# A fused attention and mixture-of-experts layer on one core: the attention's 32 token blocks split 17 and 15 around the experts instead of 16 and 16

## The chip, the cores and the metric

The kernel runs on one core of a Trainium2 chip, in one launch. The metric is the device time of that execution in microseconds. All data is fp32 but for a few 0/1 tables.

The core's engines run side by side, each through its own instruction list, and wait for each other on semaphores: TensorE (PE in the profile, with PEld for its weight loads), VectorE (DVE), ScalarE (ACT), GpSimd (POOL), and SyncE (SP), which only issues transfers here. ACT and POOL issue transfers too.

## The reference, cut to what matters

```python
x = L0_attn_x                       # 4 x 1024 tokens x 256
xn = _layernorm(x)
x = x + attn(xn) + moe(xn)
...
# attn: 16 heads of 16; each token sees itself and the 127 tokens before it (local),
#       and the means of earlier 16-token chunks (latent, 4 heads of 16)
mixed = gate * local + (1.0 - gate) * remote_h
return mixed @ out_w + out_b
...
# moe: 64 experts, 8 chosen per token, plus one shared expert
hmid = jax.nn.silu(x @ wg) * (x @ wu)
acc + cw[:, None] * (hmid @ wdn)     # for each expert; cw is 0 where it isn't chosen
```

## The kernel before

The 4096 tokens are 32 blocks of 128. Eight blocks make one batch row of 1024 tokens. The program has five parts, and every engine runs through them in the same order.

1. **Opening** (to about 106 us). Layer norm, routing scores, the choice of 8 experts for each token, and for each of the 32,768 (token, place) pairs the slot of a table `slot_rows` in DRAM, where rows lie sorted by expert.
2. **Attention, first part.** `attention(0)`: blocks 0 to 15. Meanwhile GpSimd copies normalised tokens into their slots: `scatter`, 8 indirect transfers for each of the 32 token blocks, 256 in all (line 636). They have a pace of their own (`pace`): before some of them GpSimd waits until the attention has come to a certain head pair, 15 pairs for each 4 token blocks, so 120 pairs in all. An attention block has 8 head pairs.
3. **Experts.** `experts()`: 160 rounds of two 128-row tiles. ScalarE loads the tiles from `slot_rows` (`load_pair`, line 1232) and copies gate and up weights into `wt` (`keep_weights`, line 1228); TensorE transposes the tiles (line 935), multiplies with gate and up (line 951) and with down (line 960); VectorE forms the products; GpSimd sends results to `home_rows` in DRAM, in token order (`send_home`, line 663). The first tile load needs every scatter to have landed, because any tile can hold rows of any token:

```python
for j in range(2):
    act.wait_ge(scattered[j], 16 * K * (NB // 2))
experts()
```

Before the experts VectorE also builds a table of expert numbers (`pair_row`, line 1661) and raises `words_ready`; TensorE and ScalarE wait for it, ScalarE after its first four tile loads and ahead of its first `keep_weights`.

4. **Attention, second part.** `attention(HALF)`: blocks 16 to 31. SyncE first waits for the last `send_home`, then loads 4 token blocks' rows of `home_rows` at a time, 1 MB (8 rows a token) for each token block, into a ring of four places `rows_in` in `shared_mem` (line 472), and announces each on `rows_landed`. VectorE adds them, weighted, to `x_all`: `combine` (line 1598), one instruction for each of a token's 8 rows over 128 tokens, which waits for the one before it of the same token block. 256 such instructions add everything. `add_row` places 16 of them (two token blocks) in each attention block from 17 to 31, two in each of the 8 steps; the closing call adds the last two token blocks. Block 16 adds none.
5. **End.** SyncE stores each token block once its rows and its attention result are added.

One attention block is a `body(i, ...)` on each engine, of 8 steps `s`, one for each pair of heads: TensorE `scores` (line 824, into one of two banks `psS`), VectorE `mask_pair` (lines 1542 and 1544), ScalarE `exps` (line 1116), TensorE `turn_probs` and `values` two and three steps later. Other work hangs on single steps: `project_qk(i + 1)` at 5, `latent_max` at 5 and `latent_out` at 7 on VectorE, `keep_q(i + 1, 0)` at 6. The last pieces of block i run in the first steps of block i + 1: `latent_out_turn(i)` on TensorE (line 876) at step 0, which waits for VectorE's `latent_out(i)` (line 1522), then the gate mix and the output projection. The first block of an attention part has no such tail (`tail=False`), and the call after its last block has nothing else (`live=False`). VectorE starts each block with a copy of the mask (line 1456), which marks its beginning in the trace.

Keys and values of the block before stay in SBUF (`kT`, `va`), and are moved down at each block (`shift_k`, `shift_v`), also over the experts.

## Time and profile before

| | us |
|---|---|
| median of 3 runs (lowest to highest) | 1343.48 (1343.24 to 1344.09) |
| the profiled execution's own time | 1347.35 |
| its span, first to last instruction | 1345.6 |
| TensorE busy | 1241.4 |
| VectorE busy | 958.0 |
| ScalarE busy | 862.1 |
| GpSimd busy | 641.8 |

Durations below are of the one profiled execution, whose own time is 3.87 us above the median of the runs. A start time counts from the first instruction. Where a row of the timeline has a bracket, the engine was idle for so long before it, and the name behind the arrow is what ended that; "issue" means that it waited for nothing that the profile shows. Starts of one instruction can lie a little ahead of the end printed for the one before it on the same engine, since they are pipelined.

### The profile page before, as it was taken

Reading aid. Unit: us, or ns where it says so; the run is one execution under the profiler, and the core shown is the slowest. Engines: PE = TensorE matmul, PEld = TensorE weight load, DVE = VectorE, ACT = ScalarE, POOL = GpSimd, SP = SyncE. Lnnn points to the kernel's source line nnn. Section 1 sums busy time; section 2 is a strip of 40 time slices with the busy share of each in tenths; the row PEclk is TensorE's granted clock in tenths of the full one; section 3 lists DMA queues with packets and bytes.
Section 4 is the critical chain, followed back from the end, with each engine's and each line's share of the span. In section 5 each row is a group of like instructions: output and inputs, shape, how many; then the busy total and the mean of one; then the engine's idle time right before and its main releaser. Section 6 shows DMA issues by size and latency. Waiting matters only on the chain.

```text
span 1345.6 us, 38714 instructions
## 1 busy us (share of the span) xinstructions
PE 1241.4 (92%) x9265; PEld 1169.6 (87%) x9267; DVE 958.0 (71%) x4532; ACT 862.1 (64%) x2383; POOL 641.8 (48%) x747
## 2 busy tenths in 40 slices
PE   3948999999999299999999999999999999999996
PEld 3837999999999199999999999999989898999985
DVE  6986666666666157666767676665568898989897
ACT  2416877777778165656556565666667777777774
POOL 7914777777777646656566565665620000000000
PEclk9978999999999699999999999999999999999998
DMA  8106465553333357777777777765543333323330
GB/s 252 64 34 268 165 213 182 188 184 133 120 120 109 128 168 222 227 223 228 217 235 218 216 218 229 228 197 173 169 165 106 106 105 105 105 105 107 109 119 33
DMA packets 152813, 218.40 MB, mean 162 GB/s; under 512 B 24769, under 2 KB 124866, under 8 KB 147650
## 3 DMA queue, kind: packets, MB, share of 16 engines
q1 hardware_dynamic: 80450, 86.77, 20.2%
q0 software_dynamic: 28800, 86.54, 16.8%
q10 hardware_dynamic: 43520, 44.57, 13.1%
q8 instruction: 19, 0.31, 0.1%
q14 instruction: 24, 0.20, 0.0%
HBM read 113.86 MB, written 103.81 MB: 162 GB/s over the span
## 4 chain that ended last, share of the span: by engine, by line
PE 69%; DVE 15%; issue 6%; DMA 4%; ACTq 2%; DVEq 1%; POOL 1%; ACT 1%; SPq 1%; POOLq 0%
PE psS L951 19%; PE psS L824 10%; PE psT L935 5%; PE psO L960 5%; PE psM L960 4%; PE psT L838 4%; DVE x_all L1598 4%; DMA pr<-slot_rows 3%; PE psQ L771 2%; PE psV L782 2%; PE psQ L792 2%; PE psV L811 2%; PE psT L852 2%; PE psT L851 2%; PE psT L850 1%
## 5 line engine op out<-in xcount | busy, mean ns | idle before, releaser
L951 PEld LDWEIGHTS psS<-sm,wt 128*128 128x128 f32 x2560 | 309.9, 193 | 18.6 <-issue 7.5
L951 PE MATMUL psS<-sm,wt 128*128 128x128 f32 x2560 | 315.8, 277 | 1.0 <-issue 0.2
L636 POOL DMA_INDIRECT slot_rows<-x_out_st,idx_st x256 | 256.1, 1000 | 78.6 <-issue 66.3
L1116 ACT ACTIVATE pr<-sm,nmax 128x192 f32<-128x192 f32 x512 | 205.1, 449 | 53.9 <-DVE nmax L1544 52.3
L824 PE MATMUL psS<-kT,qz 128*128 128x192 f32 x1024 | 226.3, 345 | 10.8 <-DVE qz L1487 8.4
L663 POOL DMA_INDIRECT home_rows<-qz,row_idx x160 | 154.7, 967 | 130.2 <-DVE qz L1631 101.4
L1228 ACT COPY wt<-shared_mem 128x512 f32 x320 | 183.3, 626 | 24.6 <-issue 24.6
L663 POOL DMA_INDIRECT home_rows<-sm,row_idx x160 | 155.2, 970 | 82.5 <-issue 44.4
L824 PEld LDWEIGHTS psS<-kT,qz 128*128 128x128 f32 x1024 | 165.3, 193 | 18.3 <-issue 10.7
L1216 ACT ACTIVATE prT<-psS 128x256 f32<-128x256 f32 x160 | 61.6, 385 | 185.5 <-issue 98.0
L1544 DVE CUSTOM_DVE_ANT_0 sm<-psS,pr 128x192 f32<-128x192 f32 x512 | 162.0, 354 | 23.5 <-issue 19.6
L1124 ACT COPY prT<-psT 128x384 f32<-128x384 f32 x256 | 121.9, 476 | 77.7 <-PE psT L838 74.6
L1624 DVE TENSOR_TENSOR prT<-psS,prT 128x256 f32<-128x256 f32 x160 | 67.7, 423 | 105.0 <-ACT prT L1216 104.1
L838 PE MATMUL psT<-ident,pr 128*128 128x128 f32 x768 | 125.9, 273 | 1.2 <-ACT prT L1124 1.2
L1598 DVE SCALAR_TENSOR_TENSOR x_all<-shared_mem,w,x_all (+1 forms) x256 | 123.0, 480 | 0.8
L838 PEld LDWEIGHTS psT<-ident,pr 128*128 128x128 f32 x768 | 99.9, 141 | 7.4 <-issue 2.0
L1210 ACT COPY sm<-psT 128x512 f32<-128x512 f32 x160 | 93.6, 585 | 10.5 <-PE psT L935 5.6
L935 PE MATMUL psT<-ident,pr 128*128 128x128 f32 x480 | 74.2, 278 | 24.9 <-DMA pr<-slot_rows 24.5
L1542 DVE MEMSET met<- 1x1 f32 x256 | 15.1, 59 | 100.7 <-PE psS L824 90.0
L1487 DVE TENSOR_TENSOR qz<-qT,own_head 128x1024 f32<-128x1024 f32 x64 | 78.2, 1221 | 7.3 <-ACT qT L1050 7.3
L960 PE MATMUL psO<-shared_mem,prT 128*128 x320 | 82.5, 381 | 0.2 <-DVE prT L1624 0.2
L960 PE MATMUL psM<-shared_mem,prT 128*128 x320 | 82.4, 380 | 0.0
(283 smaller groups left out, 2472.8 us busy)
## 6 DMA issues: line engine op xcount, KB each, us to landing
shared_mem<-home_rows SPq DMA_DIRECT2D x32, 1024.0 KB, 5.1
pr<-slot_rows ACTq DMA_DIRECT2D x120, 272.0 KB
qz<-slot_rows ACTq DMA_DIRECT2D x40, 272.0 KB
slot_rows<-wt SPq DMA_DIRECT2D x32, 272.0 KB
shared_mem<-in_L_ffn_We_gate SPq DMA_DIRECT2D x64, 128.0 KB
shared_mem<-in_L_ffn_We_up SPq DMA_DIRECT2D x64, 128.0 KB
shared_mem<-in_L_ffn_We_down SPq DMA_DIRECT2D x64, 128.0 KB
x_all<-in_L_attn_x SPq DMA_DIRECT2D x4, 1024.0 KB, 9.7
```

What stands on the lines that cost most here:

```text
L636: pool.indirect_dma_start(slot_rows, bass.IndirectOffsetOnAxis(ap=idx_st[:, j, k:k + 1], axis=0), x_out_st[:, j % 2, :], None).then_inc(sc ...
L663: pool.indirect_dma_start(home_rows, bass.IndirectOffsetOnAxis(ap=row_idx[:, j, a:a + 1], axis=0), ys[j][:, a, :], None).then_inc(y_out[j] ...
L824: last = mm(psS[:, p % 2, u * WIN:(u + 1) * WIN], qz[:, c, u, heads, :].rearrange("p h t -> p (h t)"), kT[:, c, u * UQ:u * UQ + WIN], star ...
L838: last = nc.tensor.transpose(psT[:, 0, a * P:(a + 1) * P], flat[:, a * P:(a + 1) * P], ident[:])
L935: last = nc.tensor.transpose(psT[:, j % 2, (a * DC + c) * P:(a * DC + c + 1) * P], xs[j][:, a, c * P:(c + 1) * P], ident[:])
L951: last = mm(psS[:, j % 2, (2 * a + n) * P:(2 * a + n + 1) * P], wt[j % 2][:, a, c, n * F:(n + 1) * F], xsT[:, j % 2, a, c, :], start=(c == ...
L960: last = mm((psM, psO)[j % 2][:, a * D:(a + 1) * D], hT[:, j % 2, a, :], ring_d[:, e % RING, :], start=True, stop=True)
L1116: nc.scalar.activation(pr[:, p % 4, par, :], sm[:, p % 4, par, :], ACT.Exp, bias=nmax[:, p % 4, par:par + 1], scale=-1.0).then_inc(probs, 1)
L1124: nc.scalar.copy(prT[:, p % 2].rearrange("p a t -> p (a t)"), psT[:, 0, 0:3 * P]).then_inc(prT_ready, 1)
L1228: last = nc.scalar.copy(wt[j % 2][:, a, :, :], ring_gu[:, e % RING, :, :])
L1544: v.tensor_tensor_reduce(sm[:, p % 4, u, :], psS[:, p % 2, u * WIN:(u + 1) * WIN], mask[:, u * WIN:(u + 1) * WIN], -1.0, -FLOOR, ALU.add, ...
L1598: ins = v.scalar_tensor_tensor(x_all[:, t, :], row, w8[:, t, k:k + 1], x_all[:, t, :], ALU.mult, ALU.add)
```

## The change

The constant HALF = 16 becomes FIRST = 17, and `attention` on TensorE, ScalarE and VectorE is given its first and last block: 0 to 16 in front of the experts, 17 to 31 behind them. The waits at the end of the first part count 17 blocks' pairs. SyncE's and GpSimd's programs are the same as before.

Blocks 18 to 31 and the closing call now have room for 30 of the 32 token blocks' rows. So block 17, the first behind the experts, adds the rows of two token blocks (0 and 1) in its last four steps: 16 instructions, four in each step, where block 16 added none. (Token block t's rows are added in the same attention block as before for every t.)

```diff
-HALF = NB // 2
+FIRST = NB // 2 + 1
...
-            def attention(start):
+            def attention(start, end):
...
-                with pe.Fori(start + 2, start + HALF - 1) as i:
+                with pe.Fori(start + 2, end - 1) as i:
                     body(i, 2)
-                body(start + HALF - 1, 2, ahead=False)
-                body(start + HALF, 2, live=False)
-                out_project(start + HALF - 1)
+                body(end - 1, 2, ahead=False)
+                body(end, 2, live=False)
+                out_project(end - 1)
...
-            attention(0)
+            attention(0, FIRST)
             pe.wait_ge(words_ready, 1)
             pe.sem_inc(pairs_done, 1)
             experts()
-            attention(HALF)
+            attention(FIRST, NB)
...
-            act.wait_ge(masked, 2 * HALF * NPAIR)
-            act.wait_ge(pv_pair, HALF * NPAIR)
+            act.wait_ge(masked, 2 * FIRST * NPAIR)
+            act.wait_ge(pv_pair, FIRST * NPAIR)
...
+                    if resuming and s >= NPAIR // 2:
+                        for n in range(2):
+                            add_row(i, 4 * s - 2 * NPAIR + n)
                     if combining:
                         add_row(i, 2 * s)
...
+                    if resuming and s >= NPAIR // 2:
+                        for n in range(2, 4):
+                            add_row(i, 4 * s - 2 * NPAIR + n)
                     if combining:
                         add_row(i, 2 * s + 1)
...
             def add_row(i, n):
-                combine(2 * (i - HALF - 1) + n // K, 2 * ((i + 1) % 2) + n // K, (n % K,))
+                combine(2 * (i - FIRST) + n // K, 2 * ((i + 1) % 2) + n // K, (n % K,))
...
-                body(start, 0, nth, tail=False, resuming=combining)
-                body(start + 1, 1, max(nth, 1), last_tail=False, combining=combining)
-                with dve.Fori(start + 2, start + HALF - 1) as i:
+                body(start, start % BPS, nth, tail=False, resuming=combining)
+                body(start + 1, start % BPS + 1, max(nth, 1), last_tail=False, combining=combining)
+                with dve.Fori(start + 2, end - 1) as i:
```

In the instruction lists TensorE, ScalarE, GpSimd and SyncE have the same rows as before; only loop bounds and awaited counts differ. VectorE's list differs in the first attention block behind the experts. There, step 5 stood so before (line 1542 and the four rows behind it are `mask_pair`, `small` and `lmax` are `latent_max`):

```order
L1542 MEMSET met 1x1
L1544 ISA sm,nmax<-psS,pr 128x192
L1544 ISA nmax 128x1
L1544 ISA sm,nmax<-psS,pr 128x192
L1544 ISA nmax 128x1
L1508 TENSOR_TENSOR small<-psM,lat_wide 128x256
L1511 TENSOR_REDUCE lmax<-small 128x4
L1513 SCALAR_TENSOR_TENSOR small<-lmax,small 128x256
```
And in the kernel after the change, with the four rows that end step 4 ahead of it:

```order
L1604 SCALAR_TENSOR_TENSOR x_all<-shared_mem,w,x_all 128x256 x4
L1542 MEMSET met 1x1
L1544 ISA sm,nmax<-psS,pr 128x192
L1544 ISA nmax 128x1
L1544 ISA sm,nmax<-psS,pr 128x192
L1544 ISA nmax 128x1
L1604 SCALAR_TENSOR_TENSOR x_all<-shared_mem,w,x_all 128x256 x2
L1508 TENSOR_TENSOR small<-psM,lat_wide 128x256
L1511 TENSOR_REDUCE lmax<-small 128x4
L1513 SCALAR_TENSOR_TENSOR small<-lmax,small 128x256
L1604 SCALAR_TENSOR_TENSOR x_all<-shared_mem,w,x_all 128x256 x2
```
The added rows (line 1604 is what was line 1598) stand ahead of `latent_max` and behind it. Step 7 of the same block, up to the mask copy that opens the next block, stood so before:

```order
L1542 MEMSET met 1x1
L1544 ISA sm,nmax<-psS,pr 128x192
L1544 ISA nmax 128x1
L1544 ISA sm,nmax<-psS,pr 128x192
L1544 ISA nmax 128x1
L1518 TENSOR_SCALAR lden<-psM 128x4
L1520 RECIPROCAL lrec<-lden 128x4
L1522 TENSOR_TENSOR lat<-psM,lrec 128x64
L1456 COPY pr<-masks 128x384
```
And after the change:

```order
L1542 MEMSET met 1x1
L1544 ISA sm,nmax<-psS,pr 128x192
L1544 ISA nmax 128x1
L1544 ISA sm,nmax<-psS,pr 128x192
L1544 ISA nmax 128x1
L1604 SCALAR_TENSOR_TENSOR x_all<-shared_mem,w,x_all 128x256 x2
L1518 TENSOR_SCALAR lden<-psM 128x4
L1520 RECIPROCAL lrec<-lden 128x4
L1522 TENSOR_TENSOR lat<-psM,lrec 128x64
L1604 SCALAR_TENSOR_TENSOR x_all<-shared_mem,w,x_all 128x256 x2
L1456 COPY pr<-masks 128x384
```
Two added rows stand ahead of `latent_out` (`lden`, `lrec`, `lat`), and two behind it.

## Rows read from the trace of the kernel before

**Rows 1.** Page, part 1: busy time, share of the span and instructions of each engine.
```profile
...
PE 1241.4 (92%) x9265; PEld 1169.6 (87%) x9267; DVE 958.0 (71%) x4532; ACT 862.1 (64%) x2383; POOL 641.8 (48%) x747
...
```

**Rows 2.** Windows: length, each engine's busy us (instructions), granted clock, DMA share, GB/s.
```profile
...
376.24:397.28 21.04, 20.84 (x157) 19.89 (x156) 13.76 (x63) 16.35 (x54) 16.43 (x19) 1.00 0.34 119
449.10:470.10 21.00, 0.00 (x0) 0.00 (x0) 0.24 (x1) 0.00 (x0) 12.47 (x13) 0.56 0.34 118
470.10:475.60 5.50, 5.50 (x25) 5.25 (x26) 0.74 (x7) 4.44 (x7) 0.00 (x0) 0.50 0.31 105
1157.02:1178.68 21.66, 21.04 (x157) 19.86 (x156) 19.41 (x79) 16.20 (x54) 0.00 (x0) 1.00 0.33 109
...
```

**Rows 3.** Timeline, VectorE (start, length, instruction, idle before): mask copies, two blocks in front.
```profile
...
376.24 0.60 DVE L1456 COPY pr<-masks 128x384 f32 x1 [0.50 <-issue]
...
397.28 0.60 DVE L1456 COPY pr<-masks 128x384 f32 x1 [0.50 <-issue]
```

**Rows 4.** Timeline, VectorE: mask copies of two blocks behind the experts.
```profile
...
1157.02 0.36 DVE L1456 COPY pr<-masks 128x384 f32 x1 [0.24 <-issue]
...
1178.68 0.36 DVE L1456 COPY pr<-masks 128x384 f32 x1 [0.24 <-issue]
```

**Rows 5.** Timeline, all engines: from the front attention's end to the experts' start.
```profile
...
445.35 0.37 ACT L1101 COPY mixedT<-psV 128x256 f32<-128x256 f32 x1 [1.70 <-PE psV L803]
...
448.66 0.42 DVE L1535 TENSOR_TENSOR x_all<-psV,x_all 128x256 f32<-128x256 f32 x1 [3.93 <-PE psV L812]
449.00 0.34 DVE L1661 SCALAR_TENSOR_TENSOR pair_row<-expert_row 1x192 int32<-1x192 int32 x1
...
464.46 0.96 POOL L636 DMA_INDIRECT slot_rows<-x_out_st,idx_st  x1 [0.30 <-issue]
467.06 1.49 ACTq L1232 DMA_DIRECT2D pr<-slot_rows  x3
468.58 0.49 ACTq L1232 DMA_DIRECT2D qz<-slot_rows  x1
...
470.10 1.97 PE L935 MATMUL psT<-ident,pr 128*128 128x128 f32 x8 [21.48 <-DMA pr<-slot_rows]
470.14 1.14 ACT L1228 COPY wt<-shared_mem 128x512 f32 x2 [24.42 <-issue]
...
```

**Rows 6.** Timeline, TensorE: the experts' first 16 gate and up matmuls.
```profile
...
471.90 3.78 PE L951 MATMUL psS<-sm,wt 128*128 128x128 f32 x16
...
```

**Rows 7.** Line 636, GpSimd's scatters, from 140 to 448 us.
```profile
...
L636 POOL DMA_INDIRECT slot_rows<-x_out_st,idx_st x231: 956/960/2002, 139.3 to 446.8; - x116
...
```

**Rows 8.** The same line from 449 to 467 us.
```profile
...
L636 POOL DMA_INDIRECT slot_rows<-x_out_st,idx_st x13: 956/960/961, 449.3 to 464.5; - x13
...
```

**Rows 9.** Timeline, VectorE: second half of block 16, then block 17's mask copy.
```profile
...
998.28 0.35 DVE L1544 CUSTOM_DVE_ANT_0 sm<-psS,pr 128x192 f32<-128x192 f32 x1 [1.44 <-issue]
...
1001.71 0.35 DVE L1544 CUSTOM_DVE_ANT_0 sm<-psS,pr 128x192 f32<-128x192 f32 x1 [1.55 <-issue]
...
1003.50 1.23 DVE L1487 TENSOR_TENSOR qz<-qT,own_head 128x1024 f32<-128x1024 f32 x1 [1.14 <-ACT qT L1050]
...
1005.61 0.23 DVE L1522 TENSOR_TENSOR lat<-psM,lrec 128x64 f32<-128x64 f32 x1
1005.75 0.35 DVE L1456 COPY pr<-masks 128x384 f32<-128x384 f32 x1
...
```

**Rows 10.** Timeline, VectorE: block 17's first two added rows, and its third pair.
```profile
...
1006.70 1.00 DVE L1598 SCALAR_TENSOR_TENSOR x_all<-shared_mem,w,x_all 128x256 f32<-128x256 f32 x2
...
1011.37 0.35 DVE L1544 CUSTOM_DVE_ANT_0 sm<-psS,pr 128x192 f32<-128x192 f32 x1 [1.14 <-issue]
...
```

**Rows 11.** Line 472: issue to landing of the load issued at 989.56 us.
```profile
...
DMA to landing us min/median/max: 4.9/4.9/4.9
```

**Rows 12.** The same of the load issued at 989.98 us.
```profile
...
DMA to landing us min/median/max: 7.5/7.5/7.5
```

**Rows 13.** Line 876, TensorE behind the experts: what ended its idle time (us, times).
```profile
...
  DVE lat L1522: 11.9, 30
...
```

More of the change, by code:

```diff
@@ L1190, in body, with attention @@
                         keep_qk(i + 1, 0, 2)
-            def attention(start):
+            def attention(start, end):
                 nth = min(start, 2)
@@ L1199, in attention @@
                 body(start + 1, max(nth, 1))
-                with act.Fori(start + 2, start + HALF - 1) as i:
+                with act.Fori(start + 2, end - 1) as i:
                     body(i, 2)
-                body(start + HALF - 1, 2, ahead=False)
-                body(start + HALF, 2, live=False)
+                body(end - 1, 2, ahead=False)
+                body(end, 2, live=False)
             def keep_tiles(j, u, first):
@@ L1261, in experts @@
                     step(j, PAIRS // XS - 1, MANY, named, final=True)
-            attention(0)
-            act.wait_ge(masked, 2 * HALF * NPAIR)
-            act.wait_ge(pv_pair, HALF * NPAIR)
+            attention(0, FIRST)
+            act.wait_ge(masked, 2 * FIRST * NPAIR)
+            act.wait_ge(pv_pair, FIRST * NPAIR)
             act.wait_ge(cleared, 16 * (E // ZROWS))
@@ L1271, in _ @@
             act.wait_ge(pairs_done, PAIRS + 1)
-            attention(HALF)
+            attention(FIRST, NB)
         @block.vector
@@ L1599, in combine, with attention @@
                     ins.then_inc(combine_steps if k < K - 1 else combined, 1)
-            def attention(start, combining):
+            def attention(start, end, combining):
                 nth = min(start, 2)
@@ L1608, in attention @@
                     dve.wait_ge(gu_ready, PAIRS)
-                body(start, 0, nth, tail=False, resuming=combining)
-                body(start + 1, 1, max(nth, 1), last_tail=False, combining=combining)
-                with dve.Fori(start + 2, start + HALF - 1) as i:
+                body(start, start % BPS, nth, tail=False, resuming=combining)
+                body(start + 1, start % BPS + 1, max(nth, 1), last_tail=False, combining=combining)
+                with dve.Fori(start + 2, end - 1) as i:
                     body(i, i % BPS, 2, combining=combining)
-                body(start + HALF - 1, BPS - 1, 2, ahead=False, combining=combining)
-                body(start + HALF, None, 2, live=False, closing=combining)
+                body(end - 1, (end - 1) % BPS, 2, ahead=False, combining=combining)
+                body(end, None, 2, live=False, closing=combining)
                 if combining:
                     dve.wait_ge(combined, NB)
-                accumulate(start + HALF - 1)
+                accumulate(end - 1)
             def make_h(j, u, first):
@@ L1676, in _ @@
             dve.wait_ge(x_biased, NB)
-            attention(0, False)
-            dve.wait_ge(probs, 2 * HALF * NPAIR)
-            dve.wait_ge(pv_pair, HALF * NPAIR)
+            attention(0, FIRST, False)
+            dve.wait_ge(probs, 2 * FIRST * NPAIR)
+            dve.wait_ge(pv_pair, FIRST * NPAIR)
             experts()
@@ L1687, in _ @@
             dve.wait_ge(weights_kept, 1)
-            attention(HALF, True)
+            attention(FIRST, NB, True)
 _INS = ['L0_attn_x', 'L0_attn_qkv_w', 'L0_attn_qkv_b', 'L0_attn_rq_w', 'L0_attn_rq_b', 'L0_attn_rkv_w', 'L0_attn_rkv_b',
```

## The prediction

> **What bounds the kernel now.** I read the page's busy times first. TensorE is busy 1241.4 us of the 1345.6 [rows 1], so about 104 us of its time are idle, and the question is which of it lies where the change acts. Then I took windows of one block in front, one behind, and of the stretch between the first attention part and the experts [rows 2]. In front TensorE is busy 20.84 of 21.04 us and VectorE 13.76: the block is TensorE's, and VectorE has some 7 us to spare. Behind, TensorE shows 21.04 and VectorE 19.41 of 21.66. From 449.1 to 470.1 TensorE and ScalarE do nothing, VectorE 0.24 us, and only GpSimd works.
>
> The mask copies give the length of a block exactly: 397.28 - 376.24 = 21.04 us in front [rows 3] and 1178.68 - 1157.02 = 21.66 us behind [rows 4].
>
> The timeline of the gap [rows 5] says what it waits for. VectorE adds block 15's result at 448.66. GpSimd's scatters go on until 464.46 + 0.96 = 465.42. At 467.06 ScalarE issues the experts' first tile loads, and the tile is there at 470.10, where TensorE ends an idle time of 21.48 us. So the gap isn't attention and isn't experts: it is the end of GpSimd's own queue. From 449 to 467 us there are 13 scatters with 960 ns each as median [rows 8].
>
> **Part 1: one more block in front.** It costs 21.04 us [rows 3] on all three engines, and it is put into a gap of 21.48 us [rows 5]. GpSimd's list is not changed, and its pacing asks for 120 head pairs, which the first 15 blocks deliver, so block 16 never holds it. What matters is which of the events that start the experts comes last now.
>
> - ScalarE's last attention copy ends at 445.35 + 0.37 = 445.72; plus 21.04 that is 466.76, before the 467.06 at which it issued tile loads.
> - The scatters now run beside a working attention to their end. There the median is 960 ns as well [rows 7], but with longer spells between: 231 starts from 139.3 to 446.8 us are 1.34 us apart, 13 starts from 449.3 to 464.5 us are 1.27 apart [rows 7, 8]. For 13 scatters that is 0.9 us: last scatter over at 466.3, tile loads from 468.0, all four issued (they took until 468.58 + 0.49 = 469.07 before [rows 5]) at 470.0, tile there at 471.0.
> - VectorE's last addition starts at 448.66 + 21.04 = 469.70, and `pair_row` [rows 5], right behind it, ends at 449.00 + 0.34 + 21.04 = 470.38. ScalarE waits for that word now, which before had been there for 20 us. It then needs what it needed before between its last load and its first weight copy, 470.14 - 469.07 = 1.07 us: 471.45 instead of 470.14, 1.31 late.
>
> So the word, not the scatters, comes last, and the first gate and up matmuls move from 471.90 [rows 6] to 473.2. Against it stands TensorE's clock. After the long pause those 16 matmuls took 3.78 us [rows 6], in a stretch with a granted clock of 0.50, which is 1.2 GHz [rows 2]. In the changed kernel TensorE comes from the attention's end with a pause of 1 to 2 us. At 2.4 GHz the set takes half, 1.9 us less, which is more than the 1.3 lost; but ScalarE's own start is 1.3 late too, so not more than that can be won back. Both ends: 0 and +1.3. I take +0.8, a little nearer to the loss, since the attention's drain has waits of its own and may leave the clock low.
>
> **Part 2: one block less behind.** That removes a steady block, 21.66 us [rows 4], since the fill, the first blocks and the closing call stay as they are. The load of rows, the additions per token block and the stores are the same work.
>
> **Part 3: 16 additions in the first block behind.** Two in a row took 1.00 us [rows 10], so 16 are 8.0 us of VectorE. In block 16, whose place block 17 takes, VectorE idled before the pair of step 5 for 1.44 us, before that of step 6 for 1.55, and before `keep_q` for 1.14 [rows 9]. Followed through: four additions in step 4 take 2.0, less 1.44: 0.56 late. Four in step 5: 0.56 + 2.0 - 1.55 = 1.01 late. In step 6 the first two lie in the wait before `keep_q`; but that wait is for ScalarE, which follows the late mask pair, so 1.01 stays; the two behind it make 2.01. In step 7 two stand ahead of `latent_out`, which ends 3.01 late; two more behind it make 4.0 at the next mask copy (at 1005.75 before [rows 9]).
>
> Who waits for VectorE there? TensorE's turn of the latent result (line 876), with the rest of the block's first step queued behind it: behind the experts its idle time was ended by `lat` 30 times, TensorE and weight loads together, 11.9 us in all [rows 13]. This is where each block ties TensorE to VectorE, so TensorE is 3.0 late. The last 1.0 falls into the idle 1.14 before the next block's third pair [rows 10]. I take +3.0. Below stands 0, if TensorE has work ahead of it at each point; above 8.0, if nothing is covered.
>
> The rows must be there in time. The first two loads took 4.9 and 7.5 us [rows 11, 12] from 989.56 and 989.98: landed at 994.5 and 997.5. Token block 0 is wanted at the end of step 4's pair, 998.28 - 1.44 = 996.8 [rows 9], token block 1 in step 6, after 1001.7. No wait.
>
> **Sum.** +0.8 - 21.66 + 3.0 = -17.9 us. Against the span: 1345.6 - 17.9 = 1327.7; the execution's own time goes from 1347.35 to 1329.5. The runs' median was 3.87 below that execution: 1343.48 - 17.9 = 1325.6.
>
> **The rivals.**
> - *The additions are not covered.* The lateness spreads into TensorE and ScalarE, and all 8.0 us count: -21.66 + 8.0 + 0.8 = -12.9, 1330.6 us. For it: the steps tie three engines together in both directions. Against it: the idle times [rows 9]. 12%.
> - *The additions are absorbed.* TensorE turns out to be bound in this block by its own work and 0 to 1 us remains: 1322.6 to 1323.6. For it: TensorE shows 20.84 of 21.04 us busy in a block in front [rows 2]. Against it: the tie at `lat`. 12%.
> - *The scatters grow longer beside a working VectorE.* Their longest in the attention was 2002 ns [rows 7], 1.04 over the median. If each of the 13 took that, the last would end 13.5 us later, and the experts would start 13.5 late: 13.5 - 21.66 + 3.0 = -5.2, 1338.3 us. Against it: the median in the attention equals the one in the gap. 6%.
> - *The other side: the scatters follow the attention.* If the queue's end is tied to the attention's end in a way that the pacing's numbers don't show, the gap stays: +21.04 - 21.66 + 3.0 = +2.4, 1345.9 us, slower than before. It decides from 18.7 us of added delay at the last scatter on. The change would then not do what it does on paper. For it: GpSimd does wait for attention events in places. Against it: 1.27 us from scatter to scatter with nothing else running shows a queue bound by itself. 3%.
> - *A new wait in the experts' first rounds,* some 5 to 8 us, 1331 to 1334: 5%.
>
> The third rival is a rule of the Trainium skill. Its page "SBUF — State Buffer", section "SBUF: two separate sides", says that VectorE and GpSimd share a port pair as an exclusive lock, and that a transfer issued from GpSimd's queue can't get its descriptors written while certain VectorE instructions run; it gives about 620 ns alone and about 3100 ns overlapped. By those figures 13 scatters would be late by some 32 us, an estimate from that page, and the kernel slower. The trace speaks against it here: 960 ns beside VectorE at 13.76 of 21.04 us busy, and 960 ns beside an idle VectorE.
>
> **How the numbers follow.** My forecast gets 62%; its own range is 1323.3 to 1327.6 (0 to 1.3 in part 1, 1.5 to 4.5 in part 3). The rivals on both sides of it reach to 1322.6 and 1330.6; with a little for another execution that makes 1321.0 to 1331.5, which leaves out the last three rivals. A time within 0.2% (2.7 us, about what a measurement of this kernel can tell from no change) needs the fourth rival: 2%. Slower by more needs it with more on top: 2%. Faster: 96%.
>
> **What the changed profile would show.** TensorE's idle time before its first line 935 instruction falls from 21.48 to about 1 us; the last scatter ends at 466 to 467 us, before the attention's last addition near 469.7; the first weight copy starts near 471.4, with `pair_row` just ahead of it; the first 16 line 951 matmuls start near 473.2, and their length says what the clock did. Behind, the first block is about 4 us longer from mask copy to mask copy than block 16 was, TensorE idles at `lat` at its end, and there is one steady block of 21.66 less. I'm wrong if scatters end after 470 us, if VectorE waits for rows in that block, or if the expert rounds are slower than before.

## The result, and the profile after

| | before | after |
|---|---|---|
| median, us (lowest to highest, 7 runs each) | 1344.79 (1343.24 to 1349.17) | 1332.89 (1329.77 to 1338.67) |
| the profiled execution's own time | 1347.35 | 1338.67 |
| its span | 1345.6 | 1336.9 |

The ratio is 0.9918 (0.9899 to 0.9937): 11.9 us faster, where 17.9 were forecast. 1332.89 us lies above the range of 1321.0 to 1331.5. The forecast of 1325.6 started from 1343.48, the median of the first 3 runs of before; over 7 runs it is 1344.79, so 1.3 of the 7.3 us that are missing lie in the starting point and 6.0 in the change.

The boundary looks as forecast in form. Timeline of the changed kernel, all engines, from the front attention's end to the experts' first rounds; it answers to [rows 5, 6]:
```profile
...
470.12 0.96 POOL L636 DMA_INDIRECT slot_rows<-x_out_st,idx_st  x1 [0.30 <-issue]
...
478.18 0.42 DVE L1535 TENSOR_TENSOR x_all<-psV,x_all 128x256 f32<-128x256 f32 x1 [4.17 <-PE psV L812]
478.52 0.34 DVE L1667 SCALAR_TENSOR_TENSOR pair_row<-expert_row 1x192 int32<-1x192 int32 x1
...
479.00 1.94 PE L935 MATMUL psT<-ident,pr 128*128 128x128 f32 x8 [0.86 <-DVE pair_row L1667]
479.93 1.14 ACT L1228 COPY wt<-shared_mem 128x512 f32 x2 [4.77 <-issue]
...
481.61 3.78 PE L951 MATMUL psS<-sm,wt 128*128 128x128 f32 x16 [0.67 <-ACT sm L1210]
...
486.03 2.77 PE L951 MATMUL psS<-sm,wt 128*128 128x128 f32 x16
```
The wait of 21.48 us is gone. The last scatter ends at 471.08, 7.1 us ahead of VectorE's last addition; the word `pair_row` comes last, and the first weight copy starts 1.75 us behind the addition's start. The whole row of events stands some 8 us later than forecast (the addition was expected near 469.7). That began in the opening, whose program the change doesn't touch. Windows of the opening and of the boundary of the changed kernel:
```profile
...
36.00:60.00 24.00, 23.30 (x115) 23.30 (x116) 14.81 (x22) 8.48 (x15) 23.41 (x33) 0.52 0.26 88
...
474.10:480.10 6.00, 4.68 (x14) 3.23 (x15) 0.68 (x2) 0.54 (x2) 0.00 (x0) 0.50 0.60 182
480.10:487.80 7.70, 7.04 (x33) 6.63 (x33) 1.81 (x15) 6.16 (x11) 0.00 (x0) 0.50 0.01 3
...
```
TensorE was granted 0.52 in the first stretch and got through 115 matmuls. The same window of the kernel before and of `e13_after_again`, a second profile of the changed kernel:
```profile
...
36.00:60.00 24.00, 23.25 (x201) 22.45 (x201) 23.62 (x28) 11.04 (x22) 23.55 (x26) 1.00 0.26 88
...
36.00:60.00 24.00, 24.00 (x152) 24.00 (x152) 16.52 (x23) 9.81 (x18) 23.54 (x30) 1.00 0.26 89
...
```
Here the matmuls say more than the granted clock. Eight of line 696 take 1.00 us in the kernel before and 1.81 in the changed one; in `e13_after_again` they take 1.81 as well until 51 us, though the record shows 1.00 throughout. The first mask copy followed at 114.63 us in the changed kernel (115 matmuls in this window), at 110.10 in `e13_after_again` (152) and at 106.41 in the kernel before (201): slow matmuls here go with a late start of the attention. `e1_before_again`, the kernel before itself, got through 131 and had its mask copy at 115.35, so a late start doesn't need the change.

At the boundary the clock is at its lower level, 1.2 GHz, through the first set of gate and up matmuls (3.78 us) and into the second (2.77 us, granted 0.69; a set takes 1.95 at 2.4 GHz).

VectorE behind the experts, answering to [rows 9, 10] (mask copies and `lat`), and TensorE's wait for `lat` [rows 13]:
```profile
...
997.41 0.35 DVE L1456 COPY pr<-masks 128x384 f32<-128x384 f32 x1
...
1017.81 0.22 DVE L1522 TENSOR_TENSOR lat<-psM,lrec 128x64 f32<-128x64 f32 x1
...
1018.87 0.35 DVE L1456 COPY pr<-masks 128x384 f32<-128x384 f32 x1
...
1038.56 0.35 DVE L1456 COPY pr<-masks 128x384 f32 x1
...
```
```profile
...
1018.09 0.33 PE L876 MATMUL psM<-ident,lat 128*128 128x128 f32 x1 [1.62 <-DVE lat L1522]
...
```
The first block behind takes 21.46 us where block 16 took 18.62: 2.84 more (4.0 forecast). VectorE waited for no rows in it, as forecast. The second takes 19.69 where 20.85 stood, so 1.16 comes back. Steady blocks are the same, 21.66 (answering to [rows 4]):
```profile
...
1104.05 0.36 DVE L1456 COPY pr<-masks 128x384 f32 x1 [0.25 <-issue]
1125.71 0.36 DVE L1456 COPY pr<-masks 128x384 f32 x1 [0.24 <-issue]
...
```
From the first mask copy to the end these two executions take 1239.2 and 1222.3 us: 16.9 less, near the forecast of 17.9. So three things are to be explained: the opening, what a typical execution of the kernel before looks like, and the rest.

### The profile page after: what moved, and what is told of

Its sections match the earlier page's. It is cut to its first block, busy times and chain, and to the rows that moved or that the text cites. A ratio compares the mean times of both kernels' runs of the same rounds, so it can differ in the third digit from the quotient of the medians.

```text
span 1336.9 us, 38681 instructions
## 1 busy us (share of the span) xinstructions
PE 1255.4 (94%) x9266; PEld 1182.4 (88%) x9267; DVE 953.3 (71%) x4532; ACT 861.7 (64%) x2383; POOL 638.7 (48%) x747
## 3 DMA queue, kind: packets, MB, share of 16 engines
q0 software_dynamic: 28800, 86.54, 16.9%
q10 hardware_dynamic: 43520, 44.57, 13.1%
## 4 chain that ended last, share of the span: by engine, by line
PE 73%; DVE 12%; issue 6%; DMA 3%; ACTq 2%; ACT 2%; DVEq 1%; SPq 1%
PE psS L951 19%; PE psS L824 10%; PE psT L935 5%; PE psO L960 5%; PE psT L838 4%; PE psM L960 4%; DVE x_all L1604 4%; DMA pr<-slot_rows 2%; PE psQ L771 2%; PE psV L811 2%; PE psV L782 2%; PE psQ L792 2%; PE psT L852 2%; PE psT L851 2%; PE psT L850 1%
## 5 line engine op out<-in xcount | busy, mean ns | idle before, releaser
L1542 DVE MEMSET met<- 1x1 f32 x256 | 15.1, 59 | 104.4 <-PE psS L824 93.8
```

## The experiments

Eight of the runs (e1 to e8) fell in a condition in which even the kernel before takes 1561 to 1581 us; they are compared only with each other. They come last here. The chip of e5 to e8 is also that of e9 to e15, so it isn't one of a certain chip. "This condition" below is the other one, in which the kernel before takes some 1345 us.

### The same kernel again, and the additions alone

`e13_after_again` is the changed kernel as it is. 

> The changed kernel, unchanged, on the same chip as the others of this call. Theory C: in the kernel before the wait ahead of the experts varies from execution to execution (21.5 us in the profiled one, 18.2 in the kernel with only the additions moved), and the moved block costs its 21.04 + 1.75 less that wait; the typical gain is 15 us, ratio 0.988 to 0.990. Theory A alone (only the changed kernel's opening was unlucky): 17 to 18 us, ratio 0.986 to 0.988.

1333.33 us against 1345.65, ratio 0.9908 (0.9878 to 0.9938): the gain repeats, and so does its size. Theory A (17 to 18 us) falls; the 15 us of theory C are more than the 12.3 measured too. What the clock takes, in the experts' first sets and behind the additions, comes out further down. In its profile the first mask copy is at 110.10, and from addition to weight copy pass 1.74 us.

`e9_additions_alone` keeps 16 blocks in front and 16 behind, and lets block 16 add 16 rows (block 17 none):
```diff
+                    if resuming and s >= NPAIR // 2:
+                        for n in range(2):
+                            add_row(i + 1, 4 * s - 2 * NPAIR + n)
...
-                body(start + 1, 1, max(nth, 1), last_tail=False, combining=combining)
+                body(start + 1, 1, max(nth, 1), last_tail=False)
```


> The kernel before (16 and 16 blocks) with block 17's 16 additions moved into the second half of block 16, block 17 adding none: the third part of the change alone. Read from the mask copies that open blocks 16, 17 and 18, 18.6 and 20.85 us apart in the kernel before. Forecast's chain (late by 4.0 at the next mask copy, 3.0 for TensorE): 22.6, then 19.7 less the 1.0 that is absorbed, sum 41.4. What the changed kernel's profile suggests (its blocks 17 and 18 took 21.45 and 19.69, with additions in both): 21.4, then 18.6 to 19.7. If the additions were absorbed: 18.6 to 19.5 for the first. Ratio 1.000 within 0.001 in each case.

Ratio 1.0023 (1.0006 to 1.0039). The two first blocks behind take 21.71 and 20.09 us, 41.80 against 39.47; the forecast's chain gave 22.6 and 18.8, so its sum (41.4) came near and its parts didn't. Part 3 alone costs 2.3 us in the trace, between "absorbed" and the 3.0 taken. A part of that is TensorE's clock. TensorE now waits 1.61 us for block 16's `lat`, where it waited for nothing before, and right behind it, over the first 3 us of block 17, the granted clock is 0.50 (1.00 in the kernel before):
```profile
...
1007.08:1010.08 3.00, 3.00 (x12) 2.79 (x12) 1.95 (x13) 2.14 (x8) 0.00 (x0) 0.50 0.61 112
...
```
Its boundary gave the clue to the failed term:
```profile
...
450.31 0.42 DVE L1535 TENSOR_TENSOR x_all<-psV,x_all 128x256 f32<-128x256 f32 x1 [3.92 <-PE psV L812]
...
468.48 2.02 PE L935 MATMUL psT<-ident,pr 128*128 128x128 f32 x8 [18.21 <-DMA pr<-slot_rows]
468.66 1.14 ACT L1228 COPY wt<-shared_mem 128x512 f32 x2 [21.37 <-issue]
...
```
Nothing was changed ahead of this place, and the wait is 18.2 us, not 21.48; from addition to weight copy 18.35 us. `e11` and `e15` below show 18.35 and 18.36.

`e10_latent_first` moves the two additions of step 7 from ahead of `latent_out` to behind it:
```diff
-                    if resuming and s >= NPAIR // 2:
+                    if resuming and NPAIR // 2 <= s < 7:
...
-                        for n in range(2, 4):
+                        for n in range(0 if s == 7 else 2, 4):
```


> The changed kernel with all four additions of step 7 of block 17 behind latent_out, where two stood ahead of it. Forecast's chain (TensorE waits for lat, so each addition ahead of it costs its full 0.5 us): the two blocks from mask copy to mask copy, 21.45 and 19.69, sum 41.14 in the changed kernel, become about 40.2. Rival (TensorE's own work or the mask pairs bound this place): the sum stays at 41.1. The ratio is that of the changed kernel.

TensorE's wait for `lat` fell from 1.62 us to 0.69:
```profile
...
1008.62 0.33 PE L876 MATMUL psM<-ident,lat 128*128 128x128 f32 x1 [0.69 <-DVE lat L1522]
...
```
The two blocks take 21.57 and 19.70 us, 41.27 against 41.15: no gain. The clock stays at 1.00 in both executions, and there the tie at `lat`, on which the forecast hung its 3.0, isn't what the additions cost. Whether the shorter wait also spares the fall of the clock that most other executions show (further down) can't be told from one profile. The run's 1331.45 (0.9901, 0.9879 to 0.9923) can't be told from the changed kernel.

### What sets the start of the experts in the kernel before

`e15_no_pacing` is the kernel before without the two lines that pace the scatters. 

> The kernel before (16 and 16) without the waits that pace GpSimd's scatters. Their idle time for attention events was 11.1 us from 140 to 448 us. If the pacing is what makes the scatters late, the last scatter ends up to 11 us earlier, the wait ahead of the experts falls from 18 to 21 us to 8 to 12, and the kernel gains 8 to 11 us, ratio 0.992 to 0.994, by which most of the change's gain would be had without moving a block. Rival (GpSimd is bound by its own 1.27 us for each scatter and catches up after each wait): the last scatter ends within 2 us of before, ratio 0.999 to 1.001.

1345.44 against 1345.65 (0.9995, 0.9979 to 1.0011): the rival held. The last scatter ends at 463.90, where `e9_additions_alone`, with the pacing, has 463.94: the scatters are bound by their own queue, not by the pacing. (Most follow each other in 1.27 us, which makes 325 us for 256; the other 15 us or so are some 30 longer steps.) The rows of the last one and of the start (here line 634 is the scatter):
```profile
...
462.94 0.96 POOL L634 DMA_INDIRECT slot_rows<-x_out_st,idx_st  x1 [0.30 <-issue]
...
468.63 1.14 ACT L1226 COPY wt<-shared_mem 128x512 f32 x2 [21.38 <-issue]
...
```
462.94 + 0.96 = 463.90, and 4.73 us later the first weight copy, as in every profile of this condition with 16 blocks in front (4.72 to 4.74). So the wait is the distance between two chains, the scatters' and the attention's, and that is set where they leave the opening. Kernel before, GpSimd's last tail clearing (line 646) and first scatter, and VectorE's first mask copy:
```profile
...
105.46 1.86 POOL L646 DMA_INDIRECT slot_rows<-shared_mem,tail_idx  x1 [0.30 <-DVE slot_idx L1442]
123.05 1.37 POOL L610 COPY idx_st<-slot_idx 128x8 uint32<-128x8 uint32 x2 [15.73 <-issue]
125.11 0.99 POOL L636 DMA_INDIRECT slot_rows<-x_out_st,idx_st  x1 [0.69 <-issue]
...
106.41 0.35 DVE L1456 COPY pr<-masks 128x384 f32<-128x384 f32 x1
...
```
The same of `e15_no_pacing`:
```profile
...
105.55 0.95 POOL L644 DMA_INDIRECT slot_rows<-shared_mem,tail_idx  x1 [0.30 <-issue]
123.09 0.32 POOL L610 COPY idx_st<-slot_idx 128x8 uint32<-128x8 uint32 x2 [16.58 <-DMA slot_rows<-shared_mem,tail_idx]
124.10 0.99 POOL L634 DMA_INDIRECT slot_rows<-x_out_st,idx_st  x1 [0.69 <-issue]
...
108.21 0.35 DVE L1454 COPY pr<-masks 128x384 f32<-128x384 f32 x1
...
```
GpSimd waits some 16 us for the cleared rows to land. In the profile of before the first scatter follows the first mask copy by 18.70 us; here by 15.89, and in no other profile of this condition by less than 15.1 or more than 16.7. Of the 2.8 us between these two executions 1.8 are an earlier attention (106.41 against 108.21) and 1.0 a later scatter (125.11 against 124.10). From first to last start the scatters then take 338 to 340 us, and the 16 blocks 342, so what differs there stays.

`e17_before_late_scatters` and `e18_after_late_scatters` test this in both kernels: GpSimd clears an unread tile 14 times ahead of its last 8 scatters.
```diff
+        unread = sb("unread", [P, 64])
...
+                if last:
+                    for _ in range(14):
+                        after(nc.gpsimd.memset(unread[:], 0.0))
```


> The kernel before, but GpSimd clears an unread 128x64 tile 14 times ahead of the last 8 scatters: some 3.1 us more in its queue (eight clears of 128x32 took 1.64 us in the opening). Nothing else. Theory A (the start of the experts follows the last scatter in the kernel before, and what varies from execution to execution is the distance between this chain and the attention's): first weight copy 4.7 us behind the last scatter, as in every profile of a 16/16 split, and 21.4 us instead of 18.35 behind the attention's last addition; time +3 us, ratio 1.002 to the kernel before. Rival (the start follows from something else, and the scatters end early enough): 18.35 us stays and the distance to the last scatter falls to 1.6 us; ratio 1.000.

> The changed kernel with the same 14 clears ahead of the last 8 scatters. Theory A: the changed kernel's start of the experts follows the word pair_row behind the attention, and its scatters end some 4.1 us earlier than they need (8.8 us ahead of the first weight copy, where 4.7 would do). So 3.1 us more change nothing: first weight copy still 1.75 us behind the attention's last addition, distance to the last scatter 5.7; ratio about 0.991, as without the clears. Rival (the scatters are still part of what the changed kernel waits for): 1.75 grows to up to 4.9, ratio up to 0.9935.

Before with late scatters: 1350.17 against 1345.81, ratio 1.0030 (1.0016 to 1.0044). The clears and the start of the experts:
```profile
...
455.65 2.88 POOL L631 MEMSET unread<- 128x64 f32 x14
459.47 0.96 POOL L640 DMA_INDIRECT slot_rows<-x_out_st,idx_st  x1 [0.94 <-POOL unread L631]
...
468.32 0.96 POOL L640 DMA_INDIRECT slot_rows<-x_out_st,idx_st  x1 [0.30 <-issue]
...
474.01 1.97 PE L939 MATMUL psT<-ident,pr 128*128 128x128 f32 x8 [21.89 <-DMA pr<-slot_rows]
...
```
The next scatter starts 4.77 us behind the one ahead of the clears (454.70) instead of 1.27, 3.5 late, and the wait is 3.5 longer than 18.35: 21.85 from addition to weight copy, which is 4.73 behind the last scatter. The kernel before follows its scatters, one for one.

The changed kernel with the same clears: 1331.62, ratio 0.9892 (0.9875 to 0.9910), no loss. Last scatter, addition, word, first transposes and first weight copy:
```profile
...
467.60 1.16 POOL L640 DMA_INDIRECT slot_rows<-x_out_st,idx_st  x1 [0.30 <-issue]
...
472.10 0.43 DVE L1539 TENSOR_TENSOR x_all<-psV,x_all 128x256 f32<-128x256 f32 x1 [4.17 <-PE psV L816]
472.44 0.34 DVE L1671 SCALAR_TENSOR_TENSOR pair_row<-expert_row 1x192 int32<-1x192 int32 x1
...
473.34 1.97 PE L939 MATMUL psT<-ident,pr 128*128 128x128 f32 x8 [1.28 <-DMA pr<-slot_rows]
473.84 1.14 ACT L1232 COPY wt<-shared_mem 128x512 f32 x2 [4.76 <-issue]
...
```
1.74 us from addition to weight copy, as without the clears. TensorE now waits for the tile again, 1.28 instead of 0.86: from the last scatter's end to the weight copy 5.08 us are left, where 4.73 is the least seen and 8.8 stood without the clears, so the 3.5 us have used up nearly all of the scatters' slack. The rival (the scatters still count) falls for this kernel, and the theory of two chains holds for both.

### The word earlier, and the opening filled

`e14_word_early` is the changed kernel with `pair_row` built ahead of the front attention; it depends on the opening alone.
```diff
             dve.wait_ge(x_biased, NB)
+            dve.wait_ge(experts_known, 16 * QT)
+            by_pair = expert_row[:].rearrange("p (u a) -> p u a", a=2)
+            v.scalar_tensor_tensor(pair_row[:], ...).then_inc(words_ready, 1)
             attention(0, FIRST)
```


> The changed kernel with the experts' number table computed ahead of the first attention part, no filling. The changed kernel starts its weight copies 1.75 us after its last front addition starts, and would start them at 0 without the word. Forecast's theory: 1.3 to 1.9 us less at the first weight copy, up to 4 us less by the third round, since TensorE's clock is better placed (3.9 us in the filled pair); ratio lower than the changed kernel's by 0.001 to 0.003. Rival: the scatters or the tile loads take the place of the word, under 0.5 us.

1330.03, ratio 0.9886 (0.9850 to 0.9923), 3.3 below the changed kernel on the same chip. The two intervals overlap, but its four runs (1328.47 to 1331.94) all lie below the five of `e13_after_again` (1332.16 to 1334.22). Its boundary:
```profile
...
471.18 1.91 PE L935 MATMUL psT<-ident,pr 128*128 128x128 f32 x8
471.33 1.14 ACT L1228 COPY wt<-shared_mem 128x512 f32 x2 [2.93 <-issue]
471.42 0.42 DVE L1535 TENSOR_TENSOR x_all<-psV,x_all 128x256 f32<-128x256 f32 x1 [4.17 <-PE psV L812]
...
473.00 2.33 PE L951 MATMUL psS<-sm,wt 128*128 128x128 f32 x16
...
475.61 1.95 PE L951 MATMUL psS<-sm,wt 128*128 128x128 f32 x16
...
```
The weight copy now starts 0.09 us ahead of the addition: 1.84 won. TensorE's higher clock comes sooner as well: the granted clock is 0.88 over the first set, where the changed kernel has 0.50, and the first two sets take 2.33 and 1.95 us instead of 3.78 and 2.77. The word did come last in the changed kernel.

`e11_before_filled` and `e19_after_filled` fill TensorE's idle time in the opening with transposes that nobody reads, meant to keep its clock up there; `e20_word_early_filled` has both edits.
```diff
+            def fill_time(n):
+                for _ in range(n):
+                    nc.tensor.transpose(psV[:, 384:512], ident[:], ident[:])
...
+            fill_time(12)
...
+                if m in (4, 5, 8):
+                    fill_time({4: 4, 5: 4, 8: 20}[m])
...
+            fill_time(32)
...
+                    fill_time(24)
```


> The kernel before with TensorE's filled opening (as in the second filled run), hoped for on a chip in the condition in which the kernel before takes 1344. Theory C (the experts of the kernel before wait for the scatters, whose chain leaves the opening by another way than the attention): filling helps the attention's start and not the scatters', so the experts start no earlier: from the end of the last front block to the first weight copy 18 to 24 us, ratio 0.998 to 1.001. Theory A alone: ratio 0.995 to 0.998.

> The changed kernel with TensorE's idle stretches of the opening filled with idle transposes into an unread bank, so that its clock doesn't fall there. The same filling did nothing for the 16/16 split (1344.74 against 1345.65). Theory B (the changed kernel's time follows the attention chain out of the opening, whose length hangs on TensorE's clock there, whereas the kernel before follows the scatter chain): the first mask copy at 107.5 to 109 us, the runs narrower than the changed kernel's 1329.8 to 1338.7, median 1329 to 1332, ratio 0.988 to 0.9905. Rival (the opening is not what spreads the changed kernel's times, or the filling costs as much as it gives): median 1333 or more, ratio 0.991 or more, as wide.

> The changed kernel with both: the word pair_row built before the attention and the opening filled. If the two are independent: the 3.3 us that the early word gave in the other kernels (1330.03 against 1333.33) on top of what the filling gives; 1326 to 1330, ratio 0.986 to 0.989. If the filling gives nothing: as the early word alone, 1330, ratio 0.9886.

| | us (lowest to highest) | ratio | first mask copy | first two blocks behind |
|---|---|---|---|---|
| e11_before_filled | 1344.74 (1343.71 to 1345.75) | 0.9988 (0.9968 to 1.0007) | 107.89 | 19.00 + 20.85 |
| e19_after_filled | 1333.39 (1328.85 to 1335.63) | 0.9902 (0.9882 to 0.9921) | 107.51 | 21.85 + 22.89 |
| e20_word_early_filled | 1330.04 (1327.98 to 1332.28) | 0.9882 (0.9865 to 0.9899) | 106.39 | 21.84 + 22.89 |

The filling gives nothing in either kernel, and `e20` comes out as the early word alone: theory C of `e11` held, my expectation for `e19` fell, although the opening was short. The profile shows where a part of it went: the second block behind takes 22.89 us, not 19.69. Windows of its beginning in `e19_after_filled`:
```profile
...
1010.62:1017.00 6.38, 6.38 (x25) 5.67 (x25) 4.45 (x17) 3.52 (x12) 0.00 (x0) 0.53 0.54 185
...
```
And the same place in `e13_after_again`, from the same mask copy:
```profile
...
1013.45:1020.00 6.55, 6.55 (x49) 6.27 (x49) 6.26 (x26) 5.51 (x18) 0.00 (x0) 1.00 0.54 185
...
```
With a granted clock of 0.53 TensorE does 25 matmuls where it does 49 at 1.00. Both executions wait 1.61 us for `lat` just before; in one the clock then falls, in the other it doesn't. Taken over all profiles: where the additions lie in the first block behind and TensorE waits 1.6 us for its `lat`, the clock over the next 3 us is 0.50 to 0.68 in ten of twelve; where it waits 0.69 us (`e10_latent_first`) or not at all (the seven without moved additions), it is 1.00 in all eight. Over the twelve profiles with 17 blocks in front (both conditions) this second block takes 19.7 us three times, 21.3 five times and 22.7 to 22.9 four times. In seven profiles with 16 in front and no moved additions it takes 20.84 to 20.86, every time.

### Where a front block is longer

In e1 to e8 a front block takes 28.3 to 29.0 us in the mean of a profile, and a steady one behind 21.66. Mask copies of `e1_before_again`, the kernel before as it is, in front and behind:
```profile
...
407.31 0.40 DVE L1456 COPY pr<-masks 128x384 f32 x1 [0.50 <-issue]
435.62 0.36 DVE L1456 COPY pr<-masks 128x384 f32 x1 [0.50 <-issue]
...
1392.43 0.36 DVE L1456 COPY pr<-masks 128x384 f32 x1 [0.24 <-issue]
1414.08 0.36 DVE L1456 COPY pr<-masks 128x384 f32 x1 [0.24 <-issue]
...
```
Its list of waits from 250 to 500 us names "remote" as what ended them:
```profile
...
ACT prT L1124 <- remote: 47.0, 16, 5.1
...
DVE met L1542 <- remote: 33.1, 11, 5.6
...
```
The three numbers are us in all, times, and the longest. Over the eight profiles there are 122 to 147 such waits each, the longest 15.2 us, and none at all in the other condition. All of them lie between the first scatter and 3 us behind the last result sent, and none between the last scatter (and 3 us behind it) and the first result: only where GpSimd issues indirect transfers. What holds the engines isn't shown, and I leave it open. With such blocks the attention ends after the scatters already with 16 blocks:
```profile
...
581.72 0.42 DVE L1535 TENSOR_TENSOR x_all<-psV,x_all 128x256 f32<-128x256 f32 x1 [4.17 <-PE psV L812]
...
583.47 1.14 ACT L1228 COPY wt<-shared_mem 128x512 f32 x2 [4.76 <-issue]
...
```
There is no wait to fill: it is 1.75 us already, as in the changed kernel. But the moved block doesn't cost 28 us either. It is the last of the front part, and by then the scatters are over. In `e2_after_again` the last one starts at 555.07; mask copies of blocks 15 and 16:
```profile
...
550.75 0.36 DVE L1456 COPY pr<-masks 128x384 f32 x1 [0.50 <-issue]
...
572.17 0.36 DVE L1456 COPY pr<-masks 128x384 f32<-128x384 f32 x1
...
```
Block 15 takes 21.42 us here (20.5 to 21.8 in the five profiles with 17 in front), and from block 16's mask copy to its addition 30.6 to 30.9 us pass in both conditions. So the moved block costs some 21 us in front and saves 21.66 behind, and what is left is the additions: the first two blocks behind take 43.3 us in the mean of these five against 39.5. (`e3`, `e6` carry the filling, `e4`, `e7` the change and the filling, `e8` the early word on top of these. In `e3` and `e4` the third stretch of the filling has 90 transposes instead of 32.)

> The kernel before, unchanged, as the yardstick for the opening (all up to the first mask copy, 106.4 us in the profiled execution of before, 114.6 in that of the changed kernel). Theory A (the shortfall is chance in the opening: executions of one program are granted TensorE's higher clock for more or less of it): ratio 1.000 within 0.003, runs spread over some 5 us, and the first mask copy may start anywhere from 104 to 115 us. Rival B (the changed program itself starts later): the first mask copy stays at 106 to 107.

> The changed kernel, unchanged. Theory A: the same attention, expert and attention stretches as before (from the first mask copy to the end 1222 us, against 1239), while the first mask copy can stand anywhere from 104 to 115 us; ratio between 0.987 and 0.993 by that chance. Rival B: the first mask copy near 114 again, ratio 0.992.

> The kernel before with TensorE kept busy in the opening by transposes of the identity that nobody reads, put where it waits anyway. Theory A: granted clock 1.0 from about 20 us on, first mask copy at 104 to 107 us, runs within 2 us of each other, ratio 0.996 to 1.000. Rival B: no less spread and the same opening as without.

> The changed kernel with the same filling. Theory A: same opening as the filled kernel of before, so that the two filled kernels differ by the change alone: 17 us (from their profiles 16 to 18), ratio 0.984 to 0.988. Rival B: the changed program still opens some 5 us or more later than the filled kernel of before, and the two differ by 11 to 12 us.

> The changed kernel, unchanged, once more, in the hope of a chip on which the kernel before takes 1344 us (on the chip of the first four runs it took 1577, with front blocks of 28 us in place of 21, so that the gap ahead of the experts was gone). Theory A (gain 17 us behind the opening, opening by chance): from the first mask copy to the end 1222 us; opening anywhere from 104 to 115. Rival B (the changed program opens later): first mask copy near 114.

> The kernel before with the filling, the second stretch of it (which had held TensorE 3 us too long) cut from 90 to 32 transposes. Theory A: first mask copy at 104 to 108 us, ratio 0.996 to 1.000 and less spread from run to run. Rival B: no change in spread.

> The changed kernel with the same filling. Theory A: same first mask copy as the filled kernel of before within 1 us, ratio lower than that one's by 0.0125 (17 us), where front blocks take 21 us. Rival B: first mask copy 5 us or more behind it, ratio lower by only 0.008. If the chip is again one with front blocks of 28 us, both theories say that the moved block costs 28 - 22 = 6 us more in front than behind, and the ratio is higher than the filled kernel of before's by 0.003 to 0.005.

> The filled changed kernel with the experts' number table (the word that ScalarE and TensorE wait for) computed ahead of the first attention part. Forecast's theory (the word is the last event ahead of the experts, 1.3 us behind the old order): TensorE's first tile transposes move up by 0.9 us and ScalarE's first weight copy by 1 to 1.8, the first round's ends by 1 to 1.5; ratio lower by 0.001. Rival (the scatters come last even so): no change.

| | us | ratio to the kernel before |
|---|---|---|
| e1_before_again | 1580.93 | 1.0016 (0.9998 to 1.0034) |
| e2_after_again | 1583.29 | 1.0023 (1.0001 to 1.0045) |
| e3_before_filled | 1579.55 | 1.0017 (0.9995 to 1.0039) |
| e4_after_filled | 1585.05 | 1.0046 (1.0025 to 1.0068) |
| e5_after_again | 1564.88 | 1.0027 (1.0011 to 1.0043) |
| e6_before_filled | 1557.44 | 0.9988 (0.9970 to 1.0006) |
| e7_after_filled | 1564.06 | 1.0014 (0.9993 to 1.0035) |
| e8_word_early | 1561.29 | 1.0002 (0.9983 to 1.0020) |

The change gains nothing there: against the partner with 16 in front its ratio is 0.001 to 0.003 higher. The terms above give -0.6 for the block and +3.9 for the additions, +3.3 us or 0.002, which fits. The 6 us that the expectation of `e7` put on the block were a wrong step, though its sign came out. Whether the kernel loses there isn't settled: the intervals of `e2` and `e5` lie above 1, but `e1`, the kernel before against itself, came out at 1.0016. The gains expected for `e2`, `e4` and `e5` didn't come, nor did the narrower spread expected of the filling (13.0 us from lowest to highest in `e3`, 11.2 in `e6`, 11.4 in `e1`). The early word again moves the weight copy from 1.75 us behind the addition to 0.09 ahead.

## Why the prediction was right or wrong

**The gap was the scatters', and a block fits into it: right.** e17 and e18 show it from both sides.

**Scatters beside a working attention: right.** The last 19 have a mean of 959 ns in the changed kernel, and no scatter of any profile took more than 2.01 us. The rival from the Trainium skill, page "SBUF — State Buffer", section "SBUF: two separate sides" (the port lock, some 3100 ns overlapped), doesn't show in any of these scatters.

**Word last: right.** Forecast 471.45 − 469.70 = 1.75 us from addition to weight copy, measured 1.75.

**+0.8 for the start of the experts: wrong, and this is the step that failed.** It compared the changed kernel with the one profiled execution of before, whose wait of 21.48 us I took as typical and corrected only by "the runs' median was 3.87 below that execution". That offset was not spread evenly. In the profiled execution the attention had left the opening 1.8 us earlier than in `e15` and the scatters 1.0 later, and so the wait was 3.1 us longer than the 18.35 that e9, e11 and e15 have. (None of the three is the kernel before as it is, but e9 is the same program up to this place.) A shorter wait is worth less when it is filled. From first mask copy to first weight copy it was 363.73 in that execution, but 360.2 to 360.4 in e9, e11 and e15; with 17 blocks it is 364.5 to 365.3. The typical term is +4.5, not +0.8 (363.73 + 0.8 would be 364.5, so the end point was right and the start was not). By parts: the block costs 21.0 us, from addition to weight copy 1.75 us stay, and a wait of 18.35 us goes. The clock that I had counted as a gain gave next to nothing: it stayed low through the first set in all five profiles (3.22 to 3.78 us) and into the second in three of them, and from weight copy to third set 8.3 to 10.0 us pass, mean 9.35, against 8.9 before: +0.5.

**−21.66 behind: right,** to 0.01.

**+3.0 for the additions: near in the mean, by luck, and wrong in the mechanism.** Where the clock stays up they cost 1.7 (41.15 against 39.47 in the first two blocks), not 3.0. But TensorE's clock falls behind the wait for `lat` in nine profiles of twelve, which the forecast didn't foresee; the mean of the two blocks is 43.1 over these twelve and 39.5 over the seven others: +3.6 (in the 1345 us condition alone 42.9 and 39.5). e10 showed that, where the clock stays up, the order around `latent_out` doesn't matter. What makes the clock fall in one execution and not in another with the same wait stays open.

**The sum with the measured terms:** +4.5 + 0.5 − 21.66 + 3.6 = −13.1 us, against −11.9 and −12.3 measured (−14.2 in e18, which should be its equal). What is left, a microsecond, is within the intervals. The rival "additions not covered" named 1330.6 and a sum of −12.9 by another mechanism; the number is near, its reason (8 us of additions) is not what happened.

**The range was too narrow** because its terms all came from one execution, and its starting point from three. With the later median of before as starting point it would have reached to 1332.8, still just below the 1332.89 measured. The opening adds a chance of its own: its first mask copy came at 106.4 to 115.4 us over the twelve profiles without filling, of either split. The profiled execution of after had one of the longest.

**A faster version:** `e14_word_early`, 1330.03 us, beats both kernels (0.9886, 0.9850 to 0.9923); `e20` with the filling is equal to it.

## What to carry to other kernels

When a change fills a wait, the wait's size is what the change is worth, and one profile gives it with the chance of that execution: a wait between two chains that part far upstream (here at 106 and 125 us, for a wait at 450) should be worked out as a difference of the two chains, and read in more than one execution. If the profiled execution is slower than the median, first ask whether some of the excess lies in the wait you are pricing. And once the wait is gone, what stood in its shadow is paid: the word behind the last addition, and the clock after a short pause.

## What the hardware did that I had not expected

- TensorE's speed in one stretch of one program, 36 to 60 us, differed from execution to execution: eight matmuls of line 696 took 1.00 or 1.81 us, and the first mask copy came up to 8.9 us later with it. The granted clock of the record was 0.52, 0.66 and 0.72 in three of the slow executions and 1.00 in others (`e13`, `e1`), so it is worth checking against the length of the matmuls.
- After the same wait of 1.61 us the clock fell in some executions and not in others, which cost up to 3.2 us (22.89 against 19.69).
- Filling an idle TensorE gave first mask copies at 106.4 to 111.0 us in eight profiles (106.4 to 115.4 in the twelve without), but no shorter run: e11 and e19 against their partners differ by 0.9 us or less, within the intervals.
- The same kernel took 1561 to 1581 us in one condition and 1345 in the other, with waits ended by "remote" of up to 5.6 us in the front attention and 15.2 us at most, all in the stretches where GpSimd issues indirect transfers.
- An indirect transfer held GpSimd for 0.96 us and left 0.30 before the next, beside a working attention as well as alone: 1.27 us each in the median. 256 of them make 325 of the 340 us of the queue that bounded the start of the experts.
